# Transposed attention scores in 64-row tiles of the array, with the layer-norm centring on ScalarE

## The reference, cut to what matters

```python
# x (32,112,256), ctx (32,375,256), mask (1,1,112,375)
qh = split_heads(layernorm(x) @ wq + bq); kh = split_heads(ctx @ wk + bk); vh = split_heads(ctx @ wv + bv)
logits = einsum('bhqd,bhkd->bhqk', qh, kh) / sqrt(16) + mask * -1e9
x = x + (einsum('bhqk,bhkd->bhqd', softmax(logits), vh) merged) @ wo + bo
xn = rms(layernorm(x)) * rms_w                 # then gate, softmax, argmax over 8 experts
x = x + score * (silu(xn @ W1[e] + b1[e]) @ W2[e] + b2[e])      # e = the token's expert
```

## Time and profile before

| | us |
|---|---|
| median of 3 runs (863.34 to 866.98) | 864.75 |
| the profiled execution, whole | 873.9 |
| the profiled execution, span from first to last instruction | 872.2 |

### The profile page before, as it was taken

How to read it: one execution, slowest core, us unless ns; L and a number is a source line. 1 busy time by engine, 2 the same in 40 slices (tenths; PEclk the granted TensorE clock), 3 DMA queues, 4 the chain that set the end, 5 groups by cost and what they waited for, 6 DMA issues and landing times.

```text
span 872.2 us, 27918 instructions
## 1 busy us (share of the span) xinstructions
PE 781.0 (90%) x8480; PEld 554.7 (64%) x8480; DVE 565.9 (65%) x1823; ACT 435.5 (50%) x1032; POOL 523.5 (60%) x753
## 2 busy tenths in 40 slices
PE   5799999999999999999999999981698988987894
PEld 4466666666666666666666666550577867776683
DVE  4667777777777777777777777638354545554352
ACT  3266666666666666666666666540323323322231
POOL 5676677677766777777677677561535435445311
PEclk9899999999999999999999999995799999999798
DMA  5776577667766876788678767605312222222110
GB/s 164 201 182 187 162 199 202 184 170 198 208 166 181 198 218 182 205 211 226 167 209 217 209 186 191 176 13 214 109 47 80 65 62 80 63 66 86 39 31 8
DMA packets 103239, 129.94 MB, mean 149 GB/s; under 512 B 12973, under 2 KB 89799, under 8 KB 102664
## 3 DMA queue, kind: packets, MB, share of 16 engines
q1 hardware_dynamic: 96744, 115.98, 49.5%
q0 software_dynamic: 5600, 12.87, 4.8%
q10 hardware_dynamic: 832, 0.27, 0.2%
HBM read 93.94 MB, written 36.06 MB: 149 GB/s over the span
## 4 chain that ended last, share of the span: by engine, by line
PE 88%; issue 5%; DVE 3%; DMA 1%; ACT 1%; ACTq 0%; POOL 0%; POOLq 0%; DVEq 0%
PE ps L1474 12%; PE ps L1454 11%; PE ps L1244 10%; PE ps L1209 10%; PE ps L1203 9%; PE ps L1260 8%; PE ps L1274 8%; PE ps L1183 5%; PE ps L1295 4%; PE ps L1323 4%; PE ps L1309 2%; PE ps L1298 1%; PE ps L1439 1%; PE ps L1194 1%; PE ps L1316 1%
## 5 line engine op out<-in xcount | busy, mean ns | idle before, releaser
L912 ACT ACTIVATE arena_b<-ps 128x448 f32<-128x448 f32 (+1 forms) x384 | 193.9, 540 | 120.4 <-PE ps L1203 87.7
L1643 DVE CUSTOM_DVE_ANT_0 arena_w<-ps,arena_w 112x375 bf16<-112x375 f32 x256 | 140.3, 548 | 78.6 <-PE ps L1183 73.8
L1070 ACT ACTIVATE arena_b<-ps,b_sb 128x256 f32<-128x256 f32 (+1 forms) x168 | 61.8, 439 | 164.0 <-PE ps L1454 103.6
L1643 DVE CUSTOM_DVE_ANT_0 arena_b<-ps,arena_w 112x375 bf16<-112x375 f32 x256 | 139.9, 546 | 0.0
L1209 PE MATMUL ps<-arena_b,arena_w 128*128 128x448 bf16 x384 | 131.6, 357 | 0.4 <-DVE arena_b L1654 0.4
L1203 PE MATMUL ps<-arena_b 128*128 128x224 f16 x768 | 131.9, 260 | 0.0
L1474 PE MATMUL ps<-arena_w,arena_b 128*128 x840 | 108.8, 284 | 24.7 <-issue 23.6
L1474 PEld LDWEIGHTS ps<-arena_w,arena_b 128*128 128x128 f16 x840 | 83.9, 101 | 46.2 <-issue 33.5
L1454 PE MATMUL ps<-arena_b,w_parts 128*128 128x256 f16 (+1 forms) x1008 | 107.2, 258 | 3.3 <-issue 3.2
L833 POOL DMA_INDIRECT arena_b<-rows,arena_b x35 | 37.3, 1066 | 108.1 <-DVE arena_b L1885 85.3
L1866 DVE TENSOR_SCALAR arena_b<-arena_b 128x512 f16<-128x512 f32 x70 | 31.1, 445 | 107.0 <-ACT arena_b L1070 88.5
(11 more groups left out here) (204 smaller groups left out, 1290.6 us busy)
## 6 DMA issues: line engine op xcount, KB each, us to landing
arena_b<-k_spill SPq DMA_DIRECT2D x128, 192.0 KB, 3.9
arena_b<-in_L_ffn_W SPq DMA_DIRECT2D x64, 256.0 KB, 4.6
arena_b<-q_spill SPq DMA_DIRECT2D x128, 112.0 KB, 4.3
k_spill<-arena_b SPq DMA_DIRECT2D x32, 384.0 KB, 2.5
arena_b<-in_ctx SPq DMA_DIRECT2D x32, 375.0 KB, 5.0
arena_w<-in_x SPq DMA_DIRECT2D x64, 112.0 KB, 4.7
q_spill<-arena_w SPq DMA_DIRECT2D x32, 224.0 KB, 2.1
rows<-arena_w SPq DMA_DIRECT2D x32, 224.0 KB, 2.3
```

The source lines that it names most:

```text
L912: nc.scalar.activation(probsT[u % PROB_BUFFERS][0:n], scoreT_bank[c][0:n, 0:QUAD * T], ACT.Exp, scale=1.0 / SCALE_SCORES).then_inc(probs_r ...
L1070: last = nc.scalar.activation(h_act[g % H_BANKS][:, i * n:(i + 1) * n], ps[:, 1 + g % H_BANKS, i * n:(i + 1) * n], ACT.Silu, bias=b1_sb[:, ...
L1643: nc.vector.tensor_tensor_reduce(out=masked_scores[r % 2], in0=shared_bank[r][0:T, 0:S], in1=mask_bias, scale=-1.0, scalar=3.4e38, op0=ALU ...
```

## The change

- **Stacks and products.** `k_stack` and `q_stack` now hold, for two quads, 64 rows each: rows 0 to 63 for the one, rows 64 to 127 for the other, with four groups of 16 rows (one head's depth, high/low by high/low) in each. Heads are no longer packed in pairs with zeros between. `scores_transposed` works on a pair of units (the same chunk of two neighbouring quads): two products for maxima and mask (128 rows, 448 columns, as before), then for each of four heads one product of 112 columns in the upper and one in the lower half of the array, eight in all. A batch has six pairs.
- **Transfers.** Reading back `k_stack` takes 8 transfers for 4, of half the size; `q_stack` takes 16 transfers for 4, and half of the bytes in all. `Q_MOVED` and `K_MOVED` follow.
- **Order on TensorE.** A step has four quarters, each begun by `scores`. Pairs 0, 2, 3 and 5 stand right behind `scores` of quads 0, 1, 2 and 3; pairs 1 and 4 right ahead of `scores` of quads 1 and 3; `values` of quads 0 and 1 run one after the other, and those of quads 2 and 3.
- **Order on ScalarE.** `exponentials` goes by pairs. `centre` moves from VectorE to ScalarE (x times 1/sigma plus a shift), and POOL makes the shift with two more small instructions in `routed_factor`.
- **Order on VectorE and POOL.** `queries_stats` comes a quarter of a step later on VectorE, `queries_rstd` comes behind `split_w2` on POOL.
- A few semaphores of the opening are merged.

```diff
-        Q_MOVED, K_MOVED = 16 * len(GROUPS), 16 * len(GROUPS)
+        Q_MOVED, K_MOVED = 4 * 16 * len(GROUPS), 2 * 16 * len(GROUPS)
...
-                    for g, (part, _) in enumerate(GROUPS):
-                        sp.dma_start(k_stack[par][32 * g:32 * g + 32].rearrange("p r j k -> p r (j k)"),
-                                     k_spill[par][part].rearrange("(r i) n -> i r n", r=PAIRS)
-                                     ).then_inc(k_stacked[par], 16)
+                    for s in range(2):
+                        for g, (part, _) in enumerate(GROUPS):
+                            sp.dma_start(k_stack[par][stack_rows(s, g)].rearrange("p h j k -> p h (j k)"),
+                                         k_spill[par][part].rearrange("(s h d) n -> s d h n", s=2, h=QUAD)[s]
+                                         ).then_inc(k_stacked[par], 16)
                     wait_apart(sp, q_spilled, 16 * (b + 1), sp_passed)
-                    for g, (_, part) in enumerate(GROUPS):
-                        sp.dma_start(q_stack[par][32 * g:32 * g + 32].rearrange("p r j a t -> p r (j a t)"),
-                                     q_spill[par][part].rearrange("(r i) n -> i r n", r=PAIRS)
-                                     ).then_inc(q_stacked[par], 16)
+                    for s in range(2):
+                        for g, (_, part) in enumerate(GROUPS):
+                            for a in range(2):
+                                sp.dma_start(q_stack[par][stack_rows(s, g)].rearrange("p (i a) j t -> p a i (j t)", a=2)[:, a],
+                                             q_spill[par][part, :, a * DT * T:(a + 1) * DT * T].rearrange(
+                                                 "(s i a d) n -> s a d i n", s=2, i=2, a=2)[s, a]
+                                             ).then_inc(q_stacked[par], 16)
...
+                pool.tensor_tensor(minus_mean2, mv2[:, 0:1], minus_one, ALU.mult).then_inc(ln2_var, 1)
...
+                pool.tensor_tensor(shift2, minus_mean2, ln2, ALU.mult).then_inc(ln2_shift, 1)
...
-                if st.exists(-2):
-                    queries_rstd(st.batch(-2), st.parity(-2))
                 if st.exists(0):
                     split_w2(st)
+                if st.exists(-2):
+                    queries_rstd(st.batch(-2), st.parity(-2))
...
+            def centre(st):
+                b, par = st.batch(3), st.parity(3)
+                act.wait_ge(ln2_shift, b + 1)
+                nc.scalar.activation(row_tile[par][:, 0:D], row_tile[par][:, D:], ACT.Identity, bias=shift2, scale=ln2
+                                     ).then_inc(centred_ready, 1)
...
+                def head(u, h, start=False, stop=False):
+                    quad, c = score_unit(u)
+                    rows = slice(P // 2 * (u % 2), P // 2 * (u % 2 + 1))
+                    return pe.matmul(scoreT_bank[u % CHUNKS][:, h * T:(h + 1) * T],
+                                     k_stack[par][rows, h, quad // 2, c * P:(c + 1) * P],
+                                     q_stack[par][rows, h, quad // 2, :], start=start, stop=stop)
...
+                    for u in units:
+                        bank_read(u)
+                        maxima_and_mask(u, True)
+                    for h in range(QUAD - 1):
+                        for u in units:
+                            head(u, h)
+                    for u in units:
+                        head(u, QUAD - 1, stop=True).then_inc(scoresT_ready, 1)
```

More of the change, by code:

```diff
@@ L492, in _, with stack_rows @@
         def _(sp):
+            def stack_rows(s, g):
+                first = P // 2 * s + DH * g
+                return slice(first, first + DH)
             def load_batch(b, parity):
@@ L994, in step @@
                 if st.exists(1):
-                    exponentials(st, 1, (0, 1, 2))
+                    exponentials(st, 1)
+                if st.exists(1):
+                    exponentials(st, 2)
                 if st.exists(-1):
@@ L1005, in step @@
                 if st.exists(3):
+                    centre(st)
                     copy_factor(st)
                 if st.exists(1):
-                    exponentials(st, 2, (0, 1, 2))
+                    exponentials(st, 3)
                 if st.exists(-1):
                     queries_high(st.batch(-1))
+                if st.exists(1):
+                    exponentials(st, 4)
                 if st.exists(-2):
@@ L1182, in scores @@
                     rows = slice(32 * r, 32 * r + 32)
[L1183 removed]
+                    mm = pe.matmul(shared_bank[r][0:T, 0:S], q_parts[par][rows, 0, a, j, :],
                                    k_parts[par][rows, 0, j, 0:S], start=True, stop=True)
@@ L1194, in transpose_maxima, with scores_transposed, bank_read, maxima_and_mask @@
                 pe.transpose(max_bank[:, 0:T], maxima, ident[0:T, 0:T]).then_inc(maxT_ready, 1)
[L1196 removed]
+            def scores_transposed(st, pair):
                 b, par = st.batch(1), st.parity(1)
[L1199 to L1212 removed]
+                units = (2 * pair, 2 * pair + 1)
+                def bank_read(u):
+                    wait_count(pe, probs_ready, UNITS * b + u - (CHUNKS - 1))
+                def maxima_and_mask(u, start):
+                    quad, c = score_unit(u)
+                    return pe.matmul(scoreT_bank[u % CHUNKS][:, 0:QUAD * T], mask_keys[:, quad, c, :],
+                                     max_rows[par].rearrange("p h t -> p (h t)"), start=start, stop=not start)
+                def head(u, h, start=False, stop=False):
+                    quad, c = score_unit(u)
+                    rows = slice(P // 2 * (u % 2), P // 2 * (u % 2 + 1))
+                    return pe.matmul(scoreT_bank[u % CHUNKS][:, h * T:(h + 1) * T],
+                                     k_stack[par][rows, h, quad // 2, c * P:(c + 1) * P],
+                                     q_stack[par][rows, h, quad // 2, :], start=start, stop=stop)
+                if pair == 0:
                     if not st.in_loop and b == 0:
@@ L1386, in step @@
                     transpose_queries(st)
+                if st.exists(1):
+                    values(st, 1, 2)
                 if st.exists(1):
@@ L1696, in step @@
                     scale_masks()
-                if st.exists(-2):
-                    queries_stats(st.batch(-2), st.parity(-2), st.half(-2))
                 if st.exists(-1):
@@ L1708, in step @@
                     first_gate_bias()
-                if st.exists(3) and (st.in_loop or st.base != B + 2):
-                    centre(st)
+                if st.exists(-2):
+                    queries_stats(st.batch(-2), st.parity(-2), st.half(-2))
                 if st.exists(-1):
@@ L1769, in _ @@
             assert done[0] == R_ONEHOT
-            centre(Step(B + 2))
             dve.wait_ge(counts_ready, 1)
```

117 lines of the change are left out of this document (47 added, 70 removed).

## The result

The changed kernel takes 1018.54 us, the median of 4 runs (1017.08 to 1022.5), beside 865.87 us for the kernel before on the same chip (4 runs, 863.34 to 870.92). The ratio is 1.176 (1.170 to 1.183), a difference of 152.7 us. The prediction said 997 us, with 935 to 1045 as the range.

What follows compares the result with a forecast made beforehand. A closed loop through SP and POOL, 21.6 us once round, was to replace TensorE's 17.18 us step: 128 us over 29 steps, plus 3.4 and 1 at start and end, 864.75 + 132 = 997 us, range 935 to 1045.

Steps and rivals of the forecast that it cites:

- The loop and what closes it: SP's `x_tail`, POOL's `residual` to `mask_queries`, SP's `q_spill` and stack loads: 15.10 us once round, 21.6 after, setting the step.
- All the signs named: Profile after: S0 (`scores` of quad 0, starting a step) waits for `mask_queries`, 11 us of issues, POOL's `x_tail` wait, lower clock.
- The terms of the loop: Parts of once round: 24 stack loads at 0.47 us add 7.6 us, the earlier landing of `x_tail` takes off 1.1.
- The start: Step 1's loads some 4 us later behind `k_spill` of batch 1; S0 of step 2 at 61.7, 3.4 us later.
- TensorE's own work: TensorE's quarters sum to 16.56 us for a step of 16.90: 0.34 us gained, worth nothing beside the loop.
- changes of shape: Switches of tile shape on TensorE, 0.13 us each: 13 in a step before, 20 after, +0.9 us.
- rival A: The loop stays under the step, issues under 0.27 us each, TensorE's gain counts: about 855 us; 5%.
- The small parts: Centring on ScalarE and later statistics lie beside other work: price zero, up to 0.5 us a step without the cover.
- B: Half-way: issues of 0.33 us and an `x_tail` landing of 2.5 us, loop 18.0 us: 890 us; 5%.
- C: Products on TensorE don't overlap and the loop is short: +0.6 us a step, 883 us; 3%.
- D: No measurable difference, gains and losses of A and C cancel; 3%.
- E: The loop is longer than forecast, small transfers issuing slower than 0.48 us or landing later: above 1045 us; 7%.

Runs made afterwards that it cites:

- e2: Kernel before with its stack loads cut into 8 and 16 transfers for 4 and 4, same bytes, nothing else changed: 984.19 us, ratio 1.181.
- e1: Changed kernel with `x_tail` issued on SP ahead of the stack loads, all 24 loads kept: 902.20 us, ratio 1.081.
- e8: Changed kernel with `x_tail` ahead of the 24 stack loads and `k_spill` ahead of the context and weight loads: 854.84 us, ratio 1.026.
- e7: Changed kernel with `q_spill` written from `q_split`, read back in 8 loads, without the masked-row factor, and `x_tail` first: 852.22 us, ratio 1.022.
- e3: Kernel before with only centring on ScalarE, the shift on POOL, `queries_stats` a quarter later, `queries_rstd` behind `split_w2`: 835.85 us, ratio 1.002.
- e7b: Changed kernel with `q_spill` written from `q_split`, read back in 8 loads, without the masked-row factor, `x_tail` behind the loads: 853.77 us, ratio 1.024.
- e4: Kernel before with `k_stack` read back in 8 loads and `q_stack` in 4 as before, same bytes: 862.38 us, ratio 1.002.

## Why the prediction was right, point by point

**The loop and what closes it: right.** The profile before read as 88% TensorE, and the step was to be set by SP's issues within SP, `x_tail`, POOL, `mask_queries`, SP. All the signs named came: 8 and 16 issues back to back for 11 us, S0 waiting with `mask_queries` as releaser, POOL 7.5 us (7 forecast) in each step for `x_tail` and no longer for ScalarE, SP's wait for `mask_queries` unchanged (148.3 us for 156 over the whole span), a lower clock. S0's own wait of 2.5 us is less than "several"; the wait of the keys' projection and the lower clock take up part of the delay. e2 shows that the issues alone are enough; e1 with e8, that opening the loop gives the time back.

**The terms of the loop: near, one missed.**

| | before | forecast | after |
|---|---|---|---|
| landing of `x_tail` until `residual` | 4.59 | 3.5 | 3.86 |
| `residual`, `context_low`, `mask_queries`, to `q_spill` | 3.88 | 3.88 | 3.81 |
| `q_spill` to the first stack load | 1.37 | 1.37 | 1.71 |
| stack loads | 3.67 | 11.3 | 11.08 |
| to the context's load, to `x_tail` | 1.59 | 1.59 | 1.61 |
| sum | 15.10 | 21.6 | 22.07 |

The stack loads are 0.46 us each for the 0.47 taken from the earlier trace rows. The Trainium skill, page "DMA: Bandwidth & Descriptors", section "Anatomy of one DMA — SWDGE (gpsimd) path", gives about 50 ns for the sequencer's part of a transfer, and it is about transfers that GpSimd issues. The stack loads are issued by SP, which that section doesn't cover. So the prediction set the figure of another path beside them; the trace of SP's queue, with 0.46 us, decides.

The time from the rows' store to the first stack load is 1.10 us in this step and 0.67 in the one before and the one behind it: the two steps of the loop's body differ, and the prediction's one row had the short one. That is 0.1 us a step on average for the time from `q_spill` to the first stack load (1.50 us for 1.37), and the landing is another 0.5 (3.99 us on average, for 3.5). So the 26 steps up to step 28 take 0.6 us more than forecast (22.20 for 21.6), and the last three less: over the 29 steps 22.01 - 21.6 = 0.4 us each, 12 us in all.

**The start: the term that was mis-sized.** S0 of step 2 came at 68.11 and not at 61.7. The prediction knew that `k_spill` of batch 1 stands behind step 0's stack loads, and gave that "some 4 us". The timelines of SP's queue before and after:

```profile
32.30 0.37 SPq L558 DMA_DIRECT2D k_spill<-arena_b  x1
...
38.93 1.75 SPq L526 DMA_DIRECT2D arena_b<-k_spill  x4
```
```profile
26.68 3.63 SPq L537 DMA_DIRECT2D arena_b<-k_spill  x8
30.44 8.63 SPq L544 DMA_DIRECT2D arena_b<-q_spill  x16
...
41.22 0.40 SPq L572 DMA_DIRECT2D k_spill<-arena_b  x1
...
46.68 5.25 SPq L537 DMA_DIRECT2D arena_b<-k_spill  x8
...
60.55 0.43 SPq L557 DMA_DIRECT2D arena_w<-in_x  x1
```

`k_spill` is 8.9 us later and its landing, awaited with nothing else to do, takes 5.4: the first stack load of step 1 moves by 7.75 us and not by 4. The eight loads of `k_stack` behind it then take 5.25 us for 3.62, another 1.6, and from `x_tail` to S0 it is 7.56 us for 6.35, another 1.2. Together these make the 6.4 us, to 0.2. This is the second loop (that of e1), which the prediction saw only as a matter of the start. It did not fall short in the steady steps, since there the first loop was longer (22.0 us for 19.0). Start 6.4 and loop 12 us are most of the 21.5 us by which 997 was low. Of the rest, 1.1 us is the median of the kernel before (865.87, where the prediction had 864.75), and some 2 us lie behind the attention, where the two profiled executions don't tell, since that of before was 8 us above its median. No two large errors made up for each other: in the loop the loads were forecast 0.2 us too long and the landing 0.5 too short.

**TensorE's own work: wrong, and of no weight only because the loop covered it.** The prediction added the quarters to 16.56 us for the step that took 16.90; with the loops open e7 has 17.65. Its terms for the products were near. A pair was to take 0.38 + 0.19 + 2 x 0.13 = 0.83 us; in e7 two products for mask and maxima take 0.49 (312.69 to 313.18), and the eight of 112 columns with their change of shape 0.31 (308.08 to 308.39), 0.80 together. So the two halves of the array do run at the same time: one after the other the eight would need 8 x 112 / 448 x 0.19 = 0.38 us in streaming alone. By the windows of e7 and of the kernel before, TensorE is busy 0.50 us a step less (477.3 us for 491.7), where the net gain was forecast as 0.34. The step that failed was the new order: the prediction counted the changes of shape in it, but moved `values` of quads 0 and 2 without naming what they covered. They covered VectorE's reading of `tail_bank`, and uncovered it costs 0.40 + 0.48 us a step in e7, most of the 1.04 us by which TensorE's idle time grew (36.7 us for 6.5 over 29 steps). Had the loop been absent, rival A's 855 us would have been wrong by its sign: e7, e7b and e8 are 2.1 to 2.7% slower than the kernel before.

**The small parts: right**, priced at nothing, and 0.2% by e3.

**What the chances came to.** Of the rivals, A fell by the issue time, B by the same (it needed 0.33 us and a landing of 2.5), C by the loop and by the eight products in 0.31 us, D and E by the result. C's 883 us (1.021 of 864.75) is what e7 shows with the loops open, 1.022, but by chance: the time went into waits for VectorE, not into the products. None of the kernels that were run beats the kernel before.

What stays open: the repair of the order (pairs in 64-row tiles with `values` of quads 0 and 2 left where they were, both loops open) was not run, so whether the 0.31 us a step would come out as a gain of about 1% isn't shown. Nor is it shown why the first steps of the kernel take longer over their issues (8.63 us for 16 loads, 5.25 for 8).

## What to carry to other kernels

Where one engine fills the chain of a pipelined kernel, look for the closed loops that run through an in-order queue from one step to the next, add up once round each, and compare the sum with the step: the difference is the spare time, and a change that splits transfers is paid for in issues (0.46 us each here, from 14 to 192 KB) from the moment that it is used up. Find all such loops before you open one, because the next longest takes its place, and often one load or store moved to another point of the queue is enough. Before a piece of work is moved on the bounding engine, name what it covers for its neighbours where it stands, and what will wait there when it is gone.

## What the runs showed of the hardware

- The issue of a transfer from SP's queue takes 0.44 to 0.46 us for 14, 28, 96 and 192 KB alike in the steps in the middle of the kernel. In the first steps of the kernel after it can take longer: 16 of 14 KB in 8.63 us, 0.54 each, and 8 of 96 KB in 5.25 us, 0.66 each.
- The landing of the 384 KB of `k_spill` goes from 2.5 us (median, before) to 4.8 us (after) and 5.0 (e1), where it is issued right behind the loads of context and weights, and is back to 2.6 when it is issued ahead of them (e8). The whole kernel moves fewer bytes after than before, 122.67 MB for 129.94.
- The granted clock over the attention (60 to 550 us) is 0.89 in the kernel after, where TensorE waits 2.5 us on average at each S0; 0.97 in e1, where its longest waits in a step are 1.5 us on average; and 1.00 in e7, where they are at most 0.6 us.
- Four chips run the kernel before in 834, 834, 860 and 866 us, with the attention at the same pace where it was compared (556.57 us to S0 of step 31 in e3 and 556.36 in e4, 556.48 in the earlier trace rows). The difference lies in the expert layer: TensorE is idle 24.7 us there ahead of the second layer's products (L1474) on the chip with 866, 14.1 on the one with 860 (e4) and 0.1 on one with 834 (e3). Why it is idle the profile doesn't say.
